# Layer 0 of a two-layer gated cross-attention block: another order of one tile's work on four engines

## What is computed

```
x = x + tanh(g_xattn[0]) * L0_xattn(layernorm(x), ctx)   # 16 heads of 16, 77 keys, bias, clip, softmax
x = x + tanh(g_ffn[0])   * L0_ffn(layernorm(x))          # top-2 mixture of 8 experts, 256 -> 1024 -> 256
x = x + tanh(g_xattn[1]) * L1_xattn(layernorm(x), ctx)   # 16 heads of 64
x = x + tanh(g_ffn[1])   * L1_ffn(layernorm(x))          # quantised: x and hidden to 16 bits, weights to 8

# L0_xattn
q, k, v = query @ Wq + bq, key_value @ Wk + bk, key_value @ Wv + bv      # per head
attn = softmax(clip(q @ k.T * scale, -1e4, 1e4))
out  = (attn @ v) @ Wo + bo

# L1_ffn: quantize_a16 divides by the largest absolute value of the whole tensor
hidden = gelu(quantize_a16(x) @ W_in_q + b_in, approximate=False)
out    = quantize_a16(hidden) @ W_out_q + b_out
```

## Time and profile before

| | |
|---|---|
| median of three runs | 1161.31 us |
| profiled execution | 1163.3 us, its span 1161.2 us |
| layer 0's cross-attention | about 0 to 246 us of the span |
| start of a plain slot to the next (four slots, 59.34 to 86.60) | 27.26 / 4 = 6.815 us |
| start of tile 3's and tile 31's subtraction (DVE 689) | 38.89 and 232.88 us |
| ffn, first and second stage | about 1015 to 1090 and 1091 to 1161 us |

### The profile page before, as it was taken

How to read it: one execution, slowest core, us unless ns; L and a number is a source line. 1 busy time by engine, 2 the same in 40 slices (tenths; PEclk the granted TensorE clock), 3 DMA queues, 4 the chain that set the end, 5 groups by cost and what they waited for, 6 DMA issues and landing times.

```text
span 1161.2 us, 26321 instructions
## 1 busy us (share of the span) xinstructions
PE 1057.4 (91%) x8919; PEld 775.3 (67%) x8919; DVE 916.9 (79%) x1960; ACT 834.7 (72%) x2382; POOL 539.4 (46%) x515
## 2 busy tenths in 40 slices
PE   6888888868969999999999999589999999889898
PEld 5666666645537777777777777357777777645477
DVE  5999999957845687666666667479999999789798
ACT  4988889836656456556556667378888888569896
POOL 5888888732252122122122111178889887500140
PEclk9999999979989999999999999889999999989899
DMA  6443334349672343333333335345252423010034
GB/s 150 118 128 110 110 110 133 123 128 284 189 206 61 53 137 90 118 101 121 124 104 120 121 115 161 112 127 161 68 158 67 154 74 92 28 38 0 1 119 137
DMA packets 128814, 132.12 MB, mean 114 GB/s; under 512 B 24792, under 2 KB 112973, under 8 KB 128557
## 3 DMA queue, kind: packets, MB, share of 16 engines
q1 hardware_dynamic: 119901, 112.17, 32.0%
q0 software_dynamic: 6480, 17.70, 5.5%
q10 hardware_dynamic: 2304, 0.59, 0.3%
HBM read 82.78 MB, written 47.64 MB: 112 GB/s over the span
## 4 chain that ended last, share of the span: by engine, by line
PE 57%; DVE 4%; ACT 4%; issue 2%; DMA 1%; POOL 1%; DVEq 0%; SPq 0%; ACTq 0%; POOLq 0%
PE exp_ps_h L1527 15%; PE exp_ps_y L1540 9%; PE a_ps_o L1953 9%; PE a_ps_sc L1937 8%; PE f_ps_h L2264 5%; PE exp_ps_y L1546 5%; PE a_ps_p L1924 3%; ACT exp_h L1590 2%; DVE f_hlo L2395 2%; PE exp_ps_x L1506 1%; PE f_ps L2447 1%; PE f_ps L2443 1%; PE f_ps_x L2255 1%; DVE all_xn L2404 1%; PE a_ps_x L1911 1%
## 5 line engine op out<-in xcount | busy, mean ns | idle before, releaser
L1590 ACT ACTIVATE exp_h<-exp_ps_h,exp_b_now 128x256 f32<-128x256 f32 (+1 forms) x320 | 124.7, 440 | 142.4 <-PE exp_ps_h L1527 142.4
L1491 POOL DMA_INDIRECT exp_xg<-xn,all_token_of x71 | 84.4, 1188 | 304.0 <-PE exp_ps_x L1506 288.5
L1527 PE MATMUL exp_ps_h<-exp_xhi,exp_w_now 128*128 128x256 bf16 (+1 forms) x1280 | 196.4, 263 | 5.9 <-DVE exp_xlo L1625 5.9
L1986 ACT ACTIVATE a_z<-a_ps_sc,a_nmx 128x77 f32<-128x77 f32 x512 | 159.3, 367 | 35.6 <-DVE a_nmx L2088 35.6
L1527 PE MATMUL exp_ps_h<-exp_xlo,exp_w_now 128*128 128x256 bf16 (+1 forms) x640 | 161.4, 263 | 0.0
L1703 DVE TENSOR_TENSOR exp_hlo<-exp_h,exp_hhi 128x512 bf16<-128x512 f32 (+1 forms) x160 | 99.4, 632 | 70.4 <-ACT exp_hhi L1597 68.5
L1540 PE MATMUL exp_ps_y<-moe_w2s,exp_hhi 128*128 x568 | 134.2, 379 | 1.3 <-DVE exp_y L1722 1.3
L1527 PEld LDWEIGHTS exp_ps_h<-exp_xhi,exp_w_now 128*128 128x128 bf16 x1280 | 120.6, 99 | 20.7 <-issue 8.3
L1986 ACT ACTIVATION_READ_ACCUMULATOR a_z<-a_ps_sc,a_nmx 128x1 f32 x512 | 127.0, 248 | 0.0
L1953 PE MATMUL a_ps_o<-a_v_now,a_phi 128*128 128x256 bf16 (+1 forms) x640 | 106.6, 272 | 2.3 <-DVE a_plo L2077 2.3
L1937 PE MATMUL a_ps_sc<-a_k_now,a_xhi 128*128 128x462 bf16 (+1 forms) x384 | 98.6, 341 | 3.4 <-DMA a_k_now<-fold_klo 2.2
(11 more groups left out here) (279 smaller groups left out, 2735.5 us busy)
## 6 DMA issues: line engine op xcount, KB each, us to landing
a_stage<-in_L_ffn_W_dram SPq DMA_DIRECT2D x64, 256.0 KB, 3.2
y_slots<-exp_y SPq DMA_DIRECT2D x71, 128.0 KB, 1.7
fold_k<-route_kst SPq DMA_DIRECT2D x16, 308.0 KB, 4.5
fold_v<-route_vst SPq DMA_DIRECT2D x16, 308.0 KB
exp_job_in<-fold_k SPq DMA_DIRECT2D x14, 352.0 KB, 3.3
exp_job_in<-fold_v SPq DMA_DIRECT2D x14, 352.0 KB, 3.3
a_x<-in_x_dram SPq DMA_DIRECT2D x32, 128.0 KB, 2.3
x<-a_xo SPq DMA_DIRECT2D x32, 128.0 KB, 1.7
```

The source lines that it names most:

```text
L1491: pool.indirect_dma_start(out=xg[:, v, u, :], out_offset=None, in_=xn_dram[:, :], in_offset=bass.IndirectOffsetOnAxis(ap=at.bitcast(U32), ...
L1527: mm = pe.matmul(hidden[:, i, f % 2, slots(j)], w1_now[:, v, k, hl, f * P:(f + 1) * P], xx[:, k, slots(j)], start=(q == 0), stop=(q == len ...
L1590: ins = act.activation(h[:, f, slots(j)], hidden[:, i, f % 2, slots(j)], ACT.Gelu_apprx_tanh, bias=b1_now[:, v, f:f + 1])
L1986: ins = act.activation(z[:, u, h * KEYS:(h + 1) * KEYS], ps_sc[:, j, (h - SB[j][0]) * KEYS:(h - SB[j][0] + 1) * KEYS], ACT.Exp, bias=nmx[: ...
```

## The change

In layer 0's cross-attention:

- PE: the queries of tile T+1 are computed at the end of slot T, before the last three matmuls of the values' product, not at the start of slot T+1. The scores stand ahead of the output product. Part 2 of the probabilities is transposed first, and then `turn_x`, then parts 0 and 1. The 17 matmuls of the values' product are grouped by the part they read: 7, 7 and 3.
- ACT: `attnT` is copied after `qT`; the last probabilities' copy comes before the two weight pieces.
- DVE: the maximum of the scores comes ahead of the residual `xo`.
- POOL: the weight remainders belong to tile T-1 and stand at the slot's start, around the power; `norm` is last.

In the ffn: the second half of the scale's chain (the step) comes after the first integers, in both stages; the constant `magic` is set earlier; in the second turn PE computes two of group 0's eight products ahead of group 1's transposes.

```diff
@@ attention, POOL slot
+                if has(T - 1):
+                    pool.wait_ge(s["hi_done"], 2 * T - 1)
...
+                    pool.tensor_tensor(w1[:, at, 1, cols], stage[:, v, 0, :], w1[:, at, 0, cols], ...
                 if has(T + 2):
                     power(T + 2, u)
+                if has(T - 1):
+                    pool.wait_ge(s["hi_done"], 2 * T)
+                    pool.tensor_tensor(w2[:, 2 * T - 2:2 * T, D:2 * D], ...
                 if has(T):
...                  # x + gbo, as before; the two remainders of tile T that stood here are gone
                 if has(T - 1):
...                  # norm, now last
@@ attention, PE slot
-                if has(T):
-                    pe.wait_ge(s["xnT_done"], T + 1)
...                  # queries of tile T
-                if has(T - 3):
-                    pe.wait_ge(s["attn_done"], T - 2)
...                  # output product
                 if has(T):
                     pe.wait_ge(s["qT_done"], T + 1)
...                  # scores
+                if has(T - 3):
+                    output(T - 3)
                 if has(T - 2):
                     pe.wait_ge(s["norm_done"], T - 1)
...
                     turn_p(T - 2, 2)
                 if has(T + 1):
                     turn_x(T + 1)
                 if has(T - 2):
...
+                    for j in range(2):
+                        wait(pe, s["pT_done"], 3 * (T - 3) + j + 1)
+                        turn_p(T - 2, j)
                     wait(pe, s["xo_done"], T - 2)
...
+                    pe.wait_ge(s["pT_done"], 3 * (T - 2) + 1)
+                    attend(T - 2, part[0])
+                    pe.wait_ge(s["pT_done"], 3 * (T - 2) + 2)
+                    attend(T - 2, part[1])
+                    pe.wait_ge(s["pT_done"], 3 * (T - 2) + 3)
+                if has(T + 1):
+                    queries(T + 1)
+                if has(T - 2):
+                    attend(T - 2, part[2]).then_inc(s["pv_done"], 1)
                 if T == 0:
                     pe.wait_ge(weights_in, 16 * N_WEIGHTS)
                     values(0, 1)
@@ ffn, first stage, DVE
-                n = steps_of(dve, s["step"], 0, ps_h[:, 1, 0:1], x_scale, tmp)
-                dve.tensor_scalar(in_step[:, :], C.wi_step[:, :], x_scale[:, 1:2], None, ALU.mult).then_inc(s["step"], 1)
+                scale_of(dve, s["step"], 0, ps_h[:, 1, 0:1], x_scale, tmp)
...
                 integers(0, 0)
+                step_of(dve, s["step"], 0, x_scale, C.wi_step, in_step)
+                dve.memset(magic[:, :], MAGIC).then_inc(s["magic_set"], 1)
@@ ffn, first stage, PE
                 def step(g, v):
+                    ahead = 2 if isinstance(g, int) and g == 1 else 0
+                    if ahead:
+                        pe.wait_ge(s["lo_done"], 2)
+                        for f in range(ahead):
+                            product(0, 0, f)
@@ ffn, second stage, ACT and DVE
-                act.wait_ge(s["magic_set"], 1)
+                act.wait_ge(C.magic_set, 1)
+                act.wait_ge(C.ffn_step, 8)
                 scale(0, 0)
+                act.wait_ge(C.ffn_step, 10)
...
                 dve.tensor_scalar(first, first, h_scale[:, 0:1], MAGIC, ALU.mult, ALU.add).then_inc(s["scaled_first"], 1)
+                step_of(dve, C.ffn_step, 5, h_scale, C.wo_step, out_step)
```

More of the change, by code:

```diff
@@ L160, in attention @@
     turns = [i for row in itertools.zip_longest(*lanes) for i in row if i is not None]
+    part = [[i for i in turns if blocks[i][0] // 4 == k] for k in range(3)]
     scale = float(dh) ** -0.5
@@ L427, in _, with queries, output, attend @@
             pe.wait_ge(keys_in, 16 * 3)
+            def queries(T):
+                pe.wait_ge(s["xnT_done"], T + 1)
+                for g in range(ng):
+                    for k in range(KD):
+                        mm = pe.matmul(ps_q[:, g * P:(g + 1) * P], wq[:, k, g * P:(g + 1) * P], xnT[:, k, :],
+                                       start=(k == 0), stop=(k == KD - 1))
+                mm.then_inc(s["q_done"], 1)
+            def output(T):
+                pe.wait_ge(s["attn_done"], T + 1)
+                for g in range(ng):
+                    mm = pe.matmul(ps_o, attnT[:, g, :], wo[:, g, :], start=(g == 0), stop=(g == ng - 1))
+                mm.then_inc(s["o_done"], 1)
+            def attend(T, some):
+                for i in some:
+                    c, q, half = blocks[i]
+                    j, g = q // ng, q % ng
+                    mine = [cc for cc, qq, _ in blocks if qq == q]
+                    n = min(P, ROWS - c * P)
+                    mm = pe.matmul(ps_v[32 * j:32 * j + 32, g * P:(g + 1) * P], vblk[0:n, T // TPB % 2, c, half, :], pT[0:n, c, :],
+                                   start=(c == mine[0]), stop=(c == mine[-1]))
+                return mm
             keys(0, 1, 0)
@@ L430, in _ @@
             pe.wait_ge(queries_in, 32)
+            queries(0)
             def slot(T, t, b):
                 u = t % 2
-                if has(T):
-                    pe.wait_ge(s["xnT_done"], T + 1)
[L436 to L440, removed]
-                if has(T - 3):
-                    pe.wait_ge(s["attn_done"], T - 2)
-                    for g in range(ng):
-                        mm = pe.matmul(ps_o, attnT[:, g, :], wo[:, g, :], start=(g == 0), stop=(g == ng - 1))
-                    mm.then_inc(s["o_done"], 1)
                 if has(T):
@@ L2259, in step @@
                         pe.wait_ge(s["lo_done"], g * 2)
-                        for f in range(FCH):
-                            wait(pe, s["gelu_done"], (g - 1) * FCH + f - 3)
-                            part = [(k, xx) for k in range(KD) for xx in (xhi, xlo)]
-                            for i, (k, xx) in enumerate(part):
-                                mm = pe.matmul(ps_h[:, f % 4, :], C.wi_q[:, k, f * P:(f + 1) * P], xx[:, 1 - v, k, :],
-                                               start=(i == 0), stop=(i == len(part) - 1))
-                            mm.then_inc(s["h_done"], 1)
+                        for f in range(ahead, FCH):
+                            product(g - 1, 1 - v, f)
                 largest(0)
@@ L2421, in _ @@
             def _(pool):
-                pool.wait_ge(s["magic_set"], 1)
+                pool.wait_ge(C.ffn_step, 8)
                 def step(g, v, n):
```

105 lines of the change are left out of this document (46 added, 59 removed).

## The result

The changed kernel took 1175.9 us (median of 4 runs, 1173.7 to 1179.1) beside 1161.5 of the kernel before; the ratio is 1.0124, 95% interval 1.0111 to 1.0137. The forecast was 1151.4 us with a range to 1157.5. The profiled execution took 1173.7 us around a span of 1171.8; the one of before had 1161.2.

The account below looks back on a forecast made before the run. A loop over several engines, not one engine, bounds the slot. Gains 13.2 (slots) + 0.4 (drain) - 3.4 (first tiles) - 0.3 (ffn) = 9.9 us: 1163.3 to 1153.4 profiled, 2.0 lower as median: 1151.4 us, range 1145.5 to 1157.5.

Parts of the forecast that it names:

- The wait for GpSimd: Layer 0's slots: VectorE's tiny line 683 waits about 0.50 us for GpSimd's remainder; the new order removes this wait.
- the four slots with keys and values: Slots building a batch's keys or values: VectorE's lines get in at `norm`'s end; 0.8 us gain, bounds -3 and +2.5.
- The last two slots: Layer 0's last two slots, no new tile prepared: about 6.2 and 5.9 us against 6.8, together 1.5 gained.
- The plain slot: Layer 0, tile 3 to 31: slot falls from 6.82 to 6.40 us, 26 slots at 0.42 giving 10.9.
- ScalarE to TensorE and back: Loop in layer 0's slot through ScalarE's copies, qT, scores, output product and transposes: 6.34 us, 6.5 with dearer hand-overs.
- Rival 2: Layer 0's ScalarE-TensorE loop is dearer, transposes starting behind a wait: slot 6.65 us, total 1159; chance 0.11.
- Rival 3: GpSimd still holds the port before VectorE's line 683: slot 6.9 us, total 1167, slower; chance 0.07.
- The score buffer's loop: Layer 0's slot, from one maximum to the next, residual now inside: 6.35 to 6.43 us.
- The first tiles: Layer 0's start: queries ahead delay the context's values and keys; 3.4 us lost at tile 3, bounds 2 and 6.
- The drain: Layer 0's last tile: values' product ends on 3 matmuls, not 10, behind the last copy; gain about 0.4 us.
- First stage: Ffn's first stage: first gelu at 1027.3 to 1028.2 against 1027.45; cost +0.1 us, bounds -0.3 and +0.8.
- Second stage: Ffn's second stage: step moved behind line 2409; cost +0.2 us, bound +0.7 if its multiplication waits for GpSimd's first scaling.

Follow-up runs that it names:

- run 6: Kernel before, with only GpSimd's two weight remainders moved a slot later; 1158.8 us, ratio 0.9974.
- run 1: Changed kernel, with the values' product in its old order over the column groups and the queries after its 7th matmul; 1159.6 us, ratio 0.9982.
- Run 11: Fastest kernel (1149.1 us), with relu ahead of attnT, output product between the transposes' two parts, residual behind xnT and shift; 1152.6 us, ratio 0.9917.
- run 5: Changed kernel, with the queries of tiles 1 and 2 again behind the context's values and keys; 1166.7 us, ratio 1.0040.
- run 4: Kernel before, with only the values' product grouped by part (7, 7 and 3 matmuls); 1161.8 us, ratio 1.0002.
- Run 8: Kernel before, with only the ffn's part of the change; 1162.4 us, ratio 1.0002.
- run 3: As run 1, with the last 10 matmuls of the values' product sorted by column group; 1165.3 us, ratio 1.0029.

## Why the prediction was wrong

**The wait for GpSimd.** Right in what goes, wrong in what it is worth: run 6 shows 0 us in a plain slot, and 3.1 us in the four slots with keys and values, where I had taken 0.8 and a bound of 2.5. (They do get in at `norm`'s end: each of their two lines is 1.0 us shorter.) The last two slots, for which I had 1.5 us, give 0.5.

**The plain slot: the step that failed.** The prediction's second loop, "ScalarE to TensorE and back", ran through ScalarE's last copy, the weight pieces and xn straight to qT, at 6.34 us. It took the queries as ready, and so left out the way from the first copy through the product and the queries to qT, which is the longest way in the changed kernel: 1.65 + 1.09 us stand in it. It has no term and no row for the product's matmuls in their new cut ahead of the queries; it put them at nothing. With 14 of them ahead of the queries, five on one column group, they take 1.65 us; with the 7 of run 1, 0.95. Then the omitted way is as long as the others, and run 1 gives 6.43 where I said 6.40: between tile 3 and tile 31 it gains 12.8 us, and the forecast was 13.2. The cut costs 17.5 us in these slots (198.73 against 181.22), of which 16.3 show in the medians.

**The rivals.** Rival 2 had the right pair of engines (ScalarE waits for TensorE) with too small a price, and another wait: it named the transposes, and ScalarE waits for the queries. Rival 3, the slower side, named GpSimd's port before line 683, and that did not happen. No rival counted the matmuls of one column group.

**The score buffer's loop.** Right as far as it was seen: 6.35 to 6.43 forecast. Run 1 stands at 6.43, and its VectorE has no wait in the loop but the one for the scores. Run 11, whose row shows the scores waiting for this loop, has 6.50: the same instructions of VectorE in another order take 2.27 us from the maximum's start to the row sums' start, not 2.20.

**The first tiles.** Right in kind, 7.25 us instead of 3.4. The forecast let TensorE be faster as it had "run longer"; it waits instead, the granted clock falls to 0.50, and the queries take twice their time (2.08 us) and the values up to 1.7 times (3.16); the keys behind them, at 1.83, are as before. How much of the 7.25 is order and how much is clock was not separated; run 5 removes both.

**The drain.** +0.50 instead of -0.4. With the old order of the values' product (run 1) the same stretch takes 13.14 us, and with the grouping alone (run 4) 13.22, so 0.3 of the 0.5 come from the grouping too; the rest was not looked for.

**The ffn.** First stage: the first gelu 0.36 us later against the scale's start, inside the bounds; but then ScalarE is not paced by TensorE for 8 gelus, which gives 1.3 us back that I had missed. Second stage: I took +0.2, the bound was +0.7, and it is +1.39. I had looked for contention at the small multiplication behind; it came at the large scaling, because GpSimd is released by the same step as VectorE and is quicker to start. Run 8 shows that the two cancel.

## What to carry to other kernels

When narrow matmuls run packed side by side in column groups, count them per group between two waits: here the busiest group's records at their own pace gave the time, in the old order and in the grouped one, and a late first record of that group made it longer (run 3). Redo this count before cutting the product by another need. A slow stretch costs only where the loop passes; test each edit of a bundle alone and in its new place, as here a free edit and a gaining edit lose together. And a stall that is large and easy to see is not the bound until the sum around each loop, with every instruction between its two ends, says so.

## What the runs showed of the hardware

- Records of the product on one column group stand 0.11 us apart, in the grouped order and in the old one; over four groups in turn the records of all together come down to 0.025 us. The product lasted as long as its busiest group: 1.65 us to the queries for 14 matmuls grouped, 1.60 for all 17 in the old order, both with five on group 2, and 0.95 with two.
- A VectorE tensor_scalar on 128x1536 took 1.28 us when it started first, 2.48 when GpSimd's scaling of the same form started 0.15 us earlier; the other way round GpSimd's took 2.02 instead of 1.55.
- With waits of 1.3 to 1.7 us between TensorE's stretches in the first 25 us, its granted clock fell to 0.50 (1.2 GHz) from 24 to 28 us; with waits under 1 us there (run 5) it stayed at 1.00.
